# Mamba, experts and window attention on one core: two products of the scan moved behind the convolution's taps, constants in the mean squares, and one DMA issued earlier

## What is computed

```python
proj = xn @ in_proj_w.T;  hs, gate = proj[..., :256], proj[..., 256:]
u = silu(conv1d(hs, conv_w, 4 taps, padding (1, 2)) + conv_b)
x_dbl = u @ x_proj_w.T                      # 64 for dt, 16 for B, 16 for C
dt, Bm, Cm = [w * (v * rsqrt(mean(v ** 2) + 1e-6)) for each part v of x_dbl]
dt = softplus(dt @ dt_proj_w.T + dt_proj_b)
h = exp(dt * A) * h + (dt * u) * Bm         # along 512 positions, for 16 states n
y = (sum over n of h * Cm + u * D) * silu(gate);  y @ out_proj_w.T
# experts: out = relu(x @ w1[e] + b1[e]) @ w2[e] + b2[e], e = argmax of the gate
# attention: 16 heads of 8, |i - j| <= 32; feed-forward: silu(gate) * up, down
```

## Time and profile before

| | |
|---|---|
| three runs, us | 1177.27, 1178.01, 1182.84 |
| median, us | 1178.01 |
| profiled execution, us | 1178.53 |
| its span, first to last instruction, us | 1176.7 |
| mean granted TensorE clock | 0.914 |
| busy: PE, DVE, ACT, POOL | 73%, 69%, 58%, 36% |

### The profile page before, as it was taken

How to read it: one execution, slowest core, us unless ns; L and a number is a source line. 1 busy time by engine, 2 the same in 40 slices (tenths; PEclk the granted TensorE clock), 3 DMA queues, 4 the chain that set the end, 5 groups by cost and what they waited for, 6 DMA issues and landing times.

```text
span 1176.7 us, 13669 instructions
## 1 busy us (share of the span) xinstructions
PE 855.9 (73%) x4346; PEld 486.1 (41%) x4346; DVE 811.7 (69%) x988; ACT 681.3 (58%) x1997; POOL 425.1 (36%) x242
## 2 busy tenths in 40 slices
PE   3553889857876887778778787778777877776772
PEld 2412667733433443344334433433334334433532
DVE  7773544569669876888688958894889687864120
ACT  2142556645775657575767576646666675674671
POOL 3174132233632462247224722472246324621000
PEclk9557999997999889998999899989989998999996
DMA  8174879853432332234223422432234324520001
GB/s 274 43 214 119 234 240 295 250 123 80 91 67 62 103 86 77 62 108 99 74 62 110 98 74 61 111 99 74 57 90 96 86 62 104 117 57 17 12 1 28
DMA packets 85304, 121.14 MB, mean 103 GB/s; under 512 B 8560, under 2 KB 43760, under 8 KB 85104
## 3 DMA queue, kind: packets, MB, share of 16 engines
q1 hardware_dynamic: 78944, 113.45, 36.1%
q0 software_dynamic: 6288, 6.82, 2.6%
HBM read 105.82 MB, written 12.32 MB: 100 GB/s over the span
## 4 chain that ended last, share of the span: by engine, by line
PE 30%; DVE 23%; issue 19%; POOL 13%; ACT 10%; DMA 4%; SPq 1%; DVEq 0%; POOLq 0%; ACTq 0%
PE y_bank L1179 11%; DVE hst L724 9%; POOL hc L1090 6%; POOL x_res L1074 3%; POOL xs_d L1058 3%; DVE dBu L716 3%; ACT pexp L993 3%; DVE z L751 2%; ACT pT L998 2%; PE work_l L1260 2%; PE work_l L1254 2%; DMA hst<-in_hidden 1%; PE work L1260 1%; PE more L1267 1%; PE work L1156 1%
## 5 line engine op out<-in xcount | busy, mean ns | idle before, releaser
L1090 POOL TENSOR_TENSOR hc<-hst,bcr 128x1024 f32<-128x1024 f32 x116 | 282.6, 2436 | 573.5 <-DVE dBu L716 573.5
L1179 PE MATMUL y_bank<-hc,pk 128*128 128x512 f32 x512 | 278.9, 672 | 85.0 <-POOL hc L1090 66.7
L724 DVE TENSOR_TENSOR_SCAN hst<-dA,dBu 128x1024 f32<-128x1024 f32 x128 | 291.5, 2277 | 3.4 <-ACT dA L909 3.1
L716 DVE TENSOR_TENSOR dBu<-dtu,bcr 128x1024 f32<-128x1024 f32 x128 | 169.5, 1324 | 30.1 <-DMA bcr<-bc_d 18.2
L1179 PEld LDWEIGHTS y_bank<-hc,pk 128*128 128x128 f32 x512 | 100.3, 207 | 199.1 <-POOL hc L1090 87.6
L909 ACT ACTIVATE dA<-dt,neg_a 128x511 f32<-128x511 f32 x256 | 170.9, 722 | 18.3 <-DVE hst L724 14.9
L993 ACT ACTIVATE pexp<-work,nmax 128x96 f32<-128x96 f32 x256 | 83.2, 339 | 10.5 <-DVE nmax L839 10.4
L993 ACT ACTIVATE pexp<-work_l,nmax 128x96 f32<-128x96 f32 x256 | 83.3, 338 | 3.1 <-DVE nmax L839 3.0
L998 ACT COPY pT<-work_l 96x512 f32<-96x512 f32 x64 | 37.2, 582 | 78.9 <-PE work_l L1260 78.2
L839 DVE TENSOR_REDUCE nmax<-work 128x4 f32<-128x384 f32 x64 | 35.4, 553 | 63.7 <-PE work L1254 63.7
L839 DVE TENSOR_REDUCE nmax<-work_l 128x4 f32<-128x384 f32 x64 | 35.5, 554 | 52.4 <-PE work_l L1254 52.4
(11 more groups left out here) (299 smaller groups left out, 1483.2 us busy)
## 6 DMA issues: line engine op xcount, KB each, us to landing
bcr<-bc_d SPq DMA_DIRECT2D x128, 512.0 KB
qbd<-in_wx SPq DMA_DIRECT2D x8, 578.0 KB, 4.3
o_all<-in_wx SPq DMA_DIRECT2D x8, 578.0 KB
pT<-in_wx SPq DMA_DIRECT2D x8, 578.0 KB
kT<-in_wx SPq DMA_DIRECT2D x8, 578.0 KB, 5.2
vw<-in_wx SPq DMA_DIRECT2D x8, 578.0 KB, 5.2
xs_d<-rbuf POOLq DMA_DIRECT2D x1, 2560.0 KB, 9.8
hst<-in_hidden SPq DMA_DIRECT2D x8, 256.0 KB, 5.9
```

The source lines that it names most:

```text
L716: v.tensor_tensor(dBu[:], dtu[par], bcr[n % RING][:, 0:1, :].to_broadcast([P, NH, L]), ALU.mult).then_inc(s_dBu, 1)
L724: v.tensor_tensor_scan(hst[n % 2][:].rearrange("p h t -> p (h t)"), dA[n % 2][:].rearrange("p h t -> p (h t)"), dBu[:].rearrange("p h t -> ...
L1090: g_.tensor_tensor(hc[n % 2][:], hst[n % 2][:], bcr[n % RING][:, 1:2, :].to_broadcast([P, NH, L]), ALU.mult).then_inc(s_hc, 1)
L1179: last = t.matmul(y_bank[h][:], ident, hc[n % 2][:, h, :], start=False, stop=(n == N - 1))
```

## The change

1. `LATE_B = {"conv1": 3, "conv3": 4}`: the product with B becomes a unit of its own in the plan (`times`). It stands behind the scan step before it, as it did, except for step 3, which now stands behind `conv1` in slot 4, and step 4, behind `conv3` in slot 6.
2. In `ss`, the product with `rms_n` and the add of epsilon become three instructions, one for each mean, with constants: ss / w + 1e-6. The semaphore s_ss counts 6 a sequence in place of 5.
3. SyncE's gathering of own heads and reciprocals moves from `rdT` to behind `spread` 0 of the scan, behind the load of the next sequence and the issue of row 3. In turns without a scan it stays where it was.

```diff
+LATE_B = {"conv1": 3, "conv3": 4}
...
             units.append(("scan", "step", n))
+            if n + 1 < N and n + 1 not in LATE_B.values():
+                units.append(("scan", "times", n + 1))
...
                     units.append((lane, name, 0))
+                if name in LATE_B:
+                    units.append(("scan", "times", LATE_B[name]))
...
+            def own_heads(b):
+                done1(sp, b, f"gate{HC - 1}")
+                done1(sp, b, f"o{G // 2 - 1}")
+                for r in range(RG):
+                    for h in range(4):
+                        q = slice(32 * r + HD * h, 32 * r + HD * h + HD)
+                        sp.dma_start(o_own[q, :], o_all[q, h, :, :].rearrange("p g q -> p (g q)")).then_inc(s_own, 16)
+                done1(sp, b, "rdT")
+                for r in range(RG):
+                    rows = rd_d[b, r] if isinstance(b, int) else rd_d[bass.ds(b, 1), r].rearrange("o h g q -> (o h) g q")
+                    sp.dma_start(rows.rearrange("h g q -> g h q"), rdenT[r * G:(r + 1) * G, :, :]).then_inc(s_rdst, 16)
+                sp.wait_ge(s_rdst, b * 64 + 64)
+                before(sp, s_out, b * 16)
...
                     if name == "spread" and k + RING - 1 < N:
                         bc_rows(b, k + RING - 1)
+                    if name == "spread" and k == 0 and b >= 2:
+                        own_heads(b - 2)
...
                     if name == "rdT":
-                        (the same lines as in own_heads)
+                        if b >= B - 2:
+                            own_heads(b)
...
-                if n + 1 < N:
-                    times_b(n + 1, b, par)
...
-                    v.tensor_tensor(ms[:], ss[:], pc("rms_n").unsqueeze(1).to_broadcast([P, NT, 3]),
-                                    ALU.mult).then_inc(s_ss, 1)
-                    dve.wait_ge(s_ss, b * 5 + 4)
-                    v.tensor_scalar(ms[:], ms[:], RMS_EPS, None, ALU.add).then_inc(s_ss, 1)
+                    dve.wait_ge(s_ss, b * 6 + 3)
+                    for k, w in enumerate((R, N, N)):
+                        v.tensor_scalar(ms[:, :, k], ss[:, :, k], 1.0 / w, RMS_EPS, ALU.mult, ALU.add).then_inc(s_ss, 1)
...
+                    elif name == "times":
+                        times_b(k, b, par)
```

More of the change, by code:

```diff
@@ L530, in bc_rows @@
                 sp.dma_start(bcr[n % RING][:], rows[:, n, :, :].to_broadcast([P, 2, L])).then_inc(s_bcr[n % RING], 16)
+            def own_heads(b):
[11 more added lines that the diff above has]
+                before(sp, s_out, b * 16)
+                rows = rd_d[b:b + 1] if isinstance(b, int) else rd_d[bass.ds(b, 1)]
+                sp.dma_start(rd_rows, rows.rearrange("o r h g q -> (o r h) (g q)").unsqueeze(1).to_broadcast(
+                    [RG * 4, HD, L])).then_inc(s_rdin, 16)
             def body(it, par):
@@ L774, in pre @@
                         v.tensor_reduce(ss[:, :, k], xsq[:, :, a:a + w], AX_X, ALU.add).then_inc(s_ss, 1)
-                    dve.wait_ge(s_ss, b * 5 + 3)
-                    v.tensor_tensor(ms[:], ss[:], pc("rms_n").unsqueeze(1).to_broadcast([P, NT, 3]),
-                                    ALU.mult).then_inc(s_ss, 1)
-                    dve.wait_ge(s_ss, b * 5 + 4)
-                    v.tensor_scalar(ms[:], ms[:], RMS_EPS, None, ALU.add).then_inc(s_ss, 1)
+                    dve.wait_ge(s_ss, b * 6 + 3)
+                    for k, w in enumerate((R, N, N)):
+                        v.tensor_scalar(ms[:, :, k], ss[:, :, k], 1.0 / w, RMS_EPS, ALU.mult, ALU.add).then_inc(s_ss, 1)
                 elif name == "xdr":
@@ L934, in pre @@
                     full0(act, b, name)
-                    before(act, s_ss, b * 5)
+                    before(act, s_ss, b * 6)
                     s.activation(xsq[:], bank0[:, 0:NT * XW].rearrange("p (j c) -> p j c", c=XW),
@@ L1105, in body @@
                     elif name == "ss":
-                        pool.wait_ge(s_ss, b * 5 + 5)
+                        pool.wait_ge(s_ss, b * 6 + 6)
                         g_.tensor_tensor(rr[:].rearrange("p j k -> p (j k)"), ms[:].rearrange("p j k -> p (j k)"),
```

## The result

| | before | after |
|---|---|---|
| median of nine runs, us | 1178.01 | 1166.75 |
| lowest and highest, us | 1174.15, 1182.84 | 1164.64, 1174.22 |
| profiled execution and its span, us | 1178.53, 1176.7 | 1171.84, 1170.1 |
| mean granted TensorE clock of it | 0.914 | 0.914 |

The ratio of the runs is 0.9927, with a 95% interval of 0.990 to 0.9954: some 8.6 us faster by the means (1177.72 and 1169.10; the medians lie 11.3 apart), where 5.1 was summed. The predicted 1173 is 6 us above the median measured; the range of 1166 to 1179 holds it. The runs of the changed kernel fall into groups by their granted clock: the two at 0.912 took 1173.91 and 1174.22, those at 0.922 and 0.923 took 1164.64 to 1166.75.

What follows compares the result with a forecast made beforehand. No single engine bounds the kernel, only the wait that ends last in each stage; 1.82 + 1.45 + 1.06 + 0.54 + 0.2 = 5.1 us off 1178.01 gives 1172.9, said as 1173, range 1166 to 1179.

Steps and rivals of the forecast that it cites:

- No wait for the row, no held tap: VectorE: dBu no longer waits for its row of B and C; taps take some 0.74 us everywhere.
- dBu 3 in the shade of ScalarE's tanh: First taps, step 3: moving dBu 3 behind tap 1 gains 0 in turns 3 to 6; the gate already waits for ScalarE.
- dBu 4, hc 3, averages, attnT, tanh for u: Turn 4, steps 4 to 5: 1.65 us gained at step 4, all but 0.26 lost through this delayed chain.
- Turn 1 and turn 7: Gains of 1.82 us in turn 1, which has no averages, and 0.54 in turn 7, which has no taps.
- rival B: Nothing is left: averages stay at 1.71 us or turns 2 and 7 meet the low clock; 1175 to 1178, chance 0.2.
- Turn 2, 1.45 us: Turn 2: u starts at 403.16 against 404.61, a gain of 1.45 us.
- Mean squares, 0.2: VectorE's ss: first of three instructions still held by POOL's hc; 0.04 us in each of six turns, 0.2 in all.
- rival A: More gets through: attnT's wait not felt, 1167, or turns 3 to 6 at the high clock, 1168; chance 0.25.
- C: Rival, slower: taps slow of themselves or held by something other than hc; 1192 us, chance 0.07.

Runs made afterwards that it cites:

- e4: Changed kernel with POOL's product of the averages one slot earlier, ahead of hc 3; 1167.87 us, ratio 0.9899 to the kernel before.
- e9: The changed kernel measured again with nothing edited; 1171.60 us, ratio 0.9946 to the kernel before.
- e2: Kernel before with only row 3 issued ahead of the own heads; 1175.33 us, ratio 0.9974 to the kernel before.
- e7: Changed kernel with dBu 3 back right behind scan step 2, dBu 4 still behind its taps; 1171.58 us, ratio 0.9962 to the kernel before.
- e6: Kernel before plus 20 products of zeros a turn on idle PE in turns 2 to 6; 1173.01 us, ratio 0.9973 to the kernel before.
- e5: Changed kernel plus 20 products of zeros a turn on idle PE in turns 2 to 6; 1167.32 us, ratio 0.9928 to the kernel before.
- e10: e4 measured again with no further edit; 1167.05 us, ratio 0.9897 to the kernel before.
- e11: Changed kernel with e4's earlier averages and e5's products of zeros together; 1158.17 us, ratio 0.9822 to the kernel before.
- e12: e11 plus three more products of zeros ahead of each sum of steps 6, 7 and 8; 1149.69 us, ratio 0.9764 to the kernel before.

## Why the prediction held, and where its size was off

- **No wait for the row, no held tap:** right. There is no such wait and the longest tap is 755 ns. The Trainium skill (SBUF — State Buffer, Who interferes with whom) calls the port pair that VectorE and GpSimd share an exclusive lock; the trace agrees, a tap has 2.85 us at most beside hc and 0.76 at most without it.
- **dBu 3 in the shade of ScalarE's tanh:** right at the low clock. Step 0 to 3 takes 20.70 us in turn 3, exactly as before.
- **dBu 4, hc 3, averages, attnT, tanh for u:** right to 0.1 us. Counted from step 0, the prediction had hc 3 at 26.83, attnT at 30.43, sg 1 at 28.35 and u at 33.86; turn 3 measured 26.83, 30.43, 28.32 and 33.93. Foretold 0.25 to 0.28 a turn, measured 0.19 and 0.22 in turns 3 and 6. e4 showed the cause by taking it away.
- **Turn 1 and turn 7:** 1.62 for 1.82 and 0.61 for 0.54 up to step 5. In turn 7 the first sum met the low clock (3.66 us for 1.98), as rival B had it, but it cost nothing by step 5.
- **Turn 2, 1.45 us:** wrong in this profile, -0.36. The prediction took over the high clock that turn 2 had before (sum 1.98 us); after, the sum met the low one. Rival B named this, at 1.5 us. In e9, the same kernel, turn 2 met the low clock again (20.70 us from step 0 to 3), in e2 and e7 the high one (19.01 and 19.04).
- **Mean squares, 0.2:** right as far as it can be seen, 0.06 us less waiting in a turn.
- **The size:** the sum of 5.1 holds the clock of each turn fixed as the one trace had it. That is the step that was mis-sized. At equal low clock the change is worth 3.4 us; where the clock is high it is worth some 7 to 9, and the profiles show one way for that: step 3 can now follow the clock by 1.7 us a turn. The prediction had both halves of this in rival A (the four turns at the high level, 5.4 us; "today the taps would stop such a gain; afterwards they don't"), and e6 against e5 showed the second. But it gave it a chance of 0.25 as one state of the kernel, where it is a share of the turns: two of the four met it in the profiled execution, 1.6 us each above the forecast. The other half of A, attnT's wait not felt, did not happen. C had nothing behind it. Two things limit this account. The 6.6 us of the profile come near the 5.1 partly by luck, since turn 2's loss of 1.8 stands against the 3.2 of turns 4 and 5. And the distance to be explained is small against the noise: the first interval is 5.4 to 11.8 us, that of e9 3.4 to 9.3, which holds the 5.1.
- **Later steps:** the prediction had nothing to say of them. In the profiled executions turns 2 to 6 together gained 7.6 us and turn 7 with what follows lost 3.8, much of it at steps whose length goes with the clock: step 9 to 10 takes between 10.4 and 14.9 us, step 13 to 14 in the changed kernel 8.6 or 10.2.

**What stays open.** Why the changed kernel meets the high clock more often: 7 of 20 runs at 0.921 or above, against 4 of 66 before. Whether that is VectorE's new order or just a shorter turn shifting the phase was not separated, and why e5's products bring so little on the change and 8.9 us on top of e4's order (e10 to e11) is open too. Nor is it settled how much of e12's gain could be had by moving real work of PE into its gaps in place of products with zeros.

## What to carry to other kernels

Read a wait against what else ends at the same place: of 34.7 us of VectorE time set free, some 3.4 reached the end while the clock was low, and the first engine to stand in the way could be named ahead from four rows. Then price the clock as a term with two values in each turn, ask which order of work could use the high one, and look at where TensorE is idle ahead of its low stretches: here that was worth 17 us (e10 to e12), twice the change. An edit that seems to bring nothing alone (e5) can be the larger half of a pair.

## What the runs showed of the hardware

- Granted clock and time go together within a kernel: for the change, runs at 0.911 to 0.914 have a mean of 1173.9 us, those at 0.921 and above one of 1165.5. Two profiles with the same mean clock (0.914) still spread their low stretches over different turns.
- Idle products are cheap and the clock is not: 145 of them (30.2 us in all), 9 a turn ahead of the sums of steps 6 to 8 included, left TensorE's busy time at 852.1 us against 856.8; the sums of hc into y_bank alone went from 275.5 to 258.0.
- The same gap of PE need not bring the same clock: in e5 it stands idle for 2.38 or 2.39 us ahead of the sum of step 7 in each of turns 2 to 6, and the clock over the 6 us from 54 us after step 0 is 1.00 in two of them and 0.59 to 0.61 in three.
- Three strided instructions of 128x4 with constants, 0.15 us each at their least, are held by POOL's product as the one with a row of constants was: 0.98 us together, ending with hc.
